# Expert 0's rows gathered from a table in DRAM, and three moves of work around the experts

## The reference

```python
topk_val, topk_idx = jax.lax.top_k(logits, TOPK)
probs = jax.nn.softmax(topk_val, axis=-1)
for kk in range(TOPK):
    idx = topk_idx[:, kk]
    w = probs[:, kk][:, None]
    for e in range(NE):
        mask = idx == e
        eo = _expert(xf, mask, ...)      # LN, 8-head attention, LN, MLP
        out = out + jnp.where(mask[:, None], eo * w, 0.0)
return out.reshape(B, N, E)
```

## Time and profile before

| what | value |
|---|---|
| median of 3 runs | 1327.05 us (1324.7 to 1328.79) |
| the profiled execution's time | 1324.23 us |
| its span | 1322.5 us |
| PE busy | 1046.1 us, 79% of the span |
| DVE busy | 741.1 us, 56% |
| ACT busy | 455.0 us, 34% |
| POOL busy | 322.1 us, 24% |
| granted TensorE clock, mean | 0.897 |

### The profile page before, as it was taken

One profiled execution on the slowest core, in us unless ns is written; L12 is line 12 of the kernel. 1 busy time (PEld: TensorE's weight loads), 2 busy tenths in 40 slices (PEclk: granted clock), 3 DMA queues, 4 the chain that ended last, 5 costly groups with the idle time before them and its releaser, 6 DMA issues.

```text
span 1322.5 us, 19279 instructions
## 1 busy us (share of the span) xinstructions
PE 1046.1 (79%) x5070; PEld 576.6 (44%) x5071; DVE 741.1 (56%) x1573; ACT 455.0 (34%) x843; POOL 322.1 (24%) x298
## 2 busy tenths in 40 slices
PE   1986799998800888778876959979799899989984
PEld 1654467777800333434333424434344344533333
DVE  5395435441461478736784473674856636736854
ACT  1301121221312366225635314434435451235522
POOL 3102324441367144203441020000000124213311
PEclk9987799998555998989897889999999999989998
DMA  5291000000427115121323020000000312120010
GB/s 148 66 285 50 1 2 0 0 0 1 157 60 233 75 48 164 42 78 32 128 85 120 1 63 1 1 0 0 0 0 3 110 48 75 41 70 1 1 31 33
DMA packets 32650, 74.58 MB, mean 56 GB/s; under 512 B 6253, under 2 KB 6551, under 8 KB 32297
## 3 DMA queue, kind: packets, MB, share of 16 engines
q1 hardware_dynamic: 24269, 55.97, 13.6%
q0 software_dynamic: 8000, 15.44, 4.0%
q10 hardware_dynamic: 288, 2.10, 0.4%
HBM read 50.63 MB, written 24.13 MB: 57 GB/s over the span
## 4 chain that ended last, share of the span: by engine, by line
PE 63%; DVE 16%; issue 10%; ACT 5%; POOL 3%; DMA 1%; DVEq 1%; SPq 0%; ACTq 0%; POOLq 0%
PE bank L1334 16%; PE bank L1425 9%; PE bank L1207 8%; PE bank L1246 5%; PE bank L1455 3%; DVE den L2159 3%; PE bank L1510 3%; PE bank L1242 2%; PE bank L1410 2%; PE bank L1389 2%; PE bank L1412 2%; PE bank L1173 2%; POOL lists L658 1%; PE bank L1469 1%; PE bank L1229 1%
## 5 line engine op out<-in xcount | busy, mean ns | idle before, releaser
L1425 PE MATMUL bank<-probs_t,v_head 128*128 128x512 f32 (+1 forms) x288 | 146.9, 593 | 17.0 <-ACT probs_t L991 16.4
L1789 DVE TENSOR_SCALAR oh_src<-iota,edge 125x1250 f16 x178 | 101.2, 568 | 105.4 <-PE bank L1207 100.5
L2072 DVE TENSOR_REDUCE mx<-bank 128x1 f32<-128x512 f32 x144 | 88.2, 656 | 75.7 <-PE bank L1389 74.9
L991 ACT ACTIVATE probs_t<-bank 128x512 f32<-128x512 f32 x144 | 81.6, 574 | 142.3 <-PE bank L1412 130.1
L560 POOL TENSOR_TENSOR w<-w_stage,w 128x1024 f16<-128x1024 f32 x40 | 85.8, 2158 | 145.9 <-ACT w L804 145.8
L1207 PE MATMUL bank<-oh_src,oh_dst 125*125 x534 | 110.8, 357 | 2.8 <-issue 0.4
L1510 PE MATMUL bank<-probs_t,v_head 128*128 128x128 f32 (+2 forms) x192 | 88.8, 549 | 6.9 <-ACT probs_t L1042 5.1
L1334 PE MATMUL bank<-hT,w 128*128 128x256 f16 (+1 forms) x552 | 89.5, 326 | 1.9 <-DVE hT L2005 1.9
L1207 PEld LDWEIGHTS bank<-oh_src,oh_dst 125*125 x534 | 70.2, 142 | 43.5 <-issue 24.2
L1455 PE MATMUL bank<-hT,w 128*128 128x512 f16 x288 | 72.7, 385 | 7.8 <-ACT t L1016 7.8
L1334 PE MATMUL bank<-w,hT 128*128 128x512 f16 x264 | 68.0, 415 | 10.3 <-DVE hT L2005 10.3
(11 more groups left out here) (306 smaller groups left out, 1956.3 us busy)
## 6 DMA issues: line engine op xcount, KB each, us to landing
w_stage<-in_ew_dram SPq DMA_DIRECT2D x40, 512.0 KB, 3.6
lists<-zeros SPq DMA_DIRECT2D x1, 10340.0 KB, 50.2
x_in<-lists SPq DMA_DIRECT2D x20, 517.0 KB, 6.7
x_mem<-lists SPq DMA_DIRECT2D x3, 1024.0 KB, 6.2
x_mem<-lists SPq DMA_DIRECT2D x1, 2560.0 KB, 10.8
out_dram<-x_mem SPq DMA_DIRECT2D x10, 250.0 KB
big<-in_x_dram SPq DMA_DIRECT2D x10, 224.0 KB
x_mem<-in_x_dram SPq DMA_DIRECT2D x1, 2240.0 KB
```

Source lines behind the costliest of these rows:

```text
L991: nc.scalar.activation(probs_t[:, x % NPB, 0:cn], stb[x % 2][:, 0:cn], ACT.Exp).then_inc(s_exp, 1)
L1425: nc.tensor.matmul(pvb[(hd * nq + s) % 2][:, 0:cn], v_head[:, hd, kt, :], probs_t[:, (hd * nx + i) % NPB, 0:cn], start=(k == 0), stop=(k = ...
L1789: nc.vector.tensor_scalar(oh_src[:, bass.ds(slot, 1), i, 0:N].rearrange("p a n -> p (a n)"), iota[:, :], edge[:, 0, i, bass.ds(g, 1)], Non ...
L2072: nc.vector.tensor_reduce(mx[:, hd, t, s:s + 1], sbk[i % 2][:, 0:cn], AX.X, ALU.max).then_inc(s_mx, 1)
```

## The change

1. **A table and a gather for expert 0.** SP writes the first 514 columns of `rows` to a DRAM `table` (10 DMAs of 125 rows, row 0 zero). DVE compares, for each tile, the slot of expert 0 that each row has with the numbers 1 to 1,280 (one-hots `where_a`, `where_b`), PE multiplies them with the rows' numbers `ids` (one column for each 128 slots), and DVE casts the result to `first_rows_i`. POOL gathers four tiles of `x_in` with it. Ahead of that gather go only 2 of the 20 scatters; the other 18 stand in expert 0's arm, ahead of `values_of`. The wait for all of them is on POOL ahead of `second_head(0)`, on DVE at the second pair, on SP ahead of the loads of x1 and of the three last list columns (`s_extra`, awaited by `owners`). `s_routed` is gone.
2. **Marks over 128 partitions.** Ten numbers a partition for each of 16 rows; the write to DRAM has 2,048 runs of 20 bytes.
3. **POOL's and SP's work.** The low halves of expert 0's six first weight pieces are made ahead of `rrstd`, the sixth piece is loaded after x2's sixth tile, most of `total_rows` is cleared early, `bias_rows`, `ones_k` and the rest of `total_rows` after the gathers. SP no longer loads `x_in` for expert 0.
4. **Short arms.** `owners` stands at the third pair (j = 2) in place of the first.
5. **Long arm.** `bias_halves` stands ahead of the maxima; PE spreads the first head's 18 score pieces over value tiles 1 to 9 in place of the last ones (`late`).

```diff
+AHEAD = 4
+SPARE = 2
@@ SP
+            sp.dma_start(table[0:1, :], zeros[0:1, 0:D + 2]).then_inc(s_lists, 16)
...
             for t in range(NT):
                 sp.wait_ge(s_x2, t + 1)
                 sp.dma_start(out_t[:, t, :], x2[:, t, :]).then_inc(s_x2out, 16)
+                if t == NB:
+                    for p in range(WB, QKV_P):
+                        load_piece(0, p)
+            sp.wait_ge(s_rn, 1)
+            sp.wait_ge(s_rr, 2)
+            sp.wait_ge(s_lists, 32)
+            for t in range(NT):
+                sp.wait_ge(s_xf, t + 1)
+                sp.dma_start(table[1 + t * TT:1 + (t + 1) * TT, :], rows[:, t, 0:D + 2]).then_inc(s_lists, 16)
             sp.wait_ge(s_marks, 1)
-            sp.dma_start(marks_dram, marks[:, :, :, :]).then_inc(s_marksout, 16)
-            for p in range(WB, QKV_P):
-                load_piece(0, p)
-            sp.wait_ge(s_x2out, 16 * NT)
+            sp.dma_start(marks_dram.rearrange("e s g (p i) -> p (e s g) i", i=PER),
+                         marks[:, :, :, :, :].rearrange("p e s g i -> p (e s g) i")).then_inc(s_marksout, 16)
             sp.wait_ge(s_marksout, 16)
-            sp.wait_ge(s_scat, 16 * 2 * NT)
-            sp.sem_inc(s_routed, 1)
...
+                sp.wait_ge(s_scat, 16 * 2 * NT)
+                with sp.If(e < 1):
+                    sp.dma_start(x_in[:, :, D + 2:DS],
+                                 lists[0:LIST, D + 2:DS].rearrange("(t p) d -> p t d", p=P)).then_inc(s_extra, 16)
...
-            load_rows(0)
@@ POOL
+            nc.gpsimd.memset(total_rows[:, 2:NTL, :], 0.0).then_inc(s_pch, 1)
...
+            for p in range(QKV_P):
+                low_weights(0, p)
+            pool.wait_ge(s_rmv, 1)
...
-            nc.gpsimd.memset(total_rows[:, :, :], 0.0).then_inc(s_econst, 1)
...
-            for p in range(QKV_P):
-                low_weights(0, p)
-            pool.wait_ge(s_routed, 1)
+            pool.wait_ge(s_lists, 32)
+            scatter(range(SPARE // 2))
+            pool.wait_ge(s_lists, 32 + 16 * NT)
+            pool.wait_ge(s_index, 1)
+            gather(range(AHEAD))
+            nc.gpsimd.memset(total_rows[:, 0:2, :], 0.0).then_inc(s_econst, 1)
...
+                with nc.gpsimd.If(e < 1):
+                    if nt > AHEAD:
+                        pool.wait_ge(s_index, 2)
+                        gather(range(AHEAD, nt))
+                    scatter(range(SPARE // 2, NT))
...
                     values_of(0, 1)
+                    pool.wait_ge(s_scat, 16 * 2 * NT)
                     second_head(0)
@@ PE
+            for i in range(AHEAD):
+                last = tokens_of(i, where_a, i * P, 0)
...
-                    late = max(2, nt // 2)
                     for t in range(1, nt):
                         value(t)
-                        if t >= late:
-                            for i in range((t - late) * nx // (nt - late), (t + 1 - late) * nx // (nt - late)):
-                                scores(0, i)
+                        for i in range((t - 1) * nx // (nt - 1), t * nx // (nt - 1)):
+                            scores(0, i)
@@ DVE
+            one_hots_of(where_a, 0, LW_A)
...
+            dve.wait_ge(s_placed, 1)
+            token_rows(0, AHEAD)
+            one_hots_of(where_b, LW_A, LW_B)
+            one_hots_of(where_a, LW_A + LW_B, LW_B)
...
+                    if j == 1:
+                        dve.wait_ge(s_scat, 16 * 2 * NT)
...
-                    if j == 0:
+                    if j == 2:
                         owners(e, nt)
...
                     split_pair()
+                    bias_halves()
                     for i in range(nx):
                         maximum(0, i)
                     owners(e, nt)
                     second_head_copies()
-                    bias_halves()
+                    dve.wait_ge(s_scat, 16 * 2 * NT)
```

More of the change, by code:

```diff
@@ L58 @@
 UP = 5
+AHEAD = 4
+SPARE = 2
+PER = LW // P
+LW_A = AHEAD * P
+LW_B = (LW - LW_A) // 2
 FAR = -30000.0
@@ L169, in program @@
         lists = dram("lists", (NE * LIST, DS), F32)
+        table = dram("table", (N + 1, D + 2), F32)
         ident = sb("ident", [P, P], F32)
@@ L272, in program @@
         gaps = sb("gaps", [P, 3, NE], F32, route)
-        marks = sb("marks", [NE, 2, 2, LW], F16, route)
+        where_a = sb("where_a", [TT, NT, LW_A], F16, route)
+        where_b = sb("where_b", [TT, NT, LW_B], F16, route)
+        number = sb("number", [TT, LW], F16, route)
+        ids = sb("ids", [TT, NT], F16, route)
+        where = sb("where", [TT, 3, NT], F32, route)
+        first_rows_i = sb("first_rows_i", [P, NTL], I32, route)
         route.close()
@@ L439, in program @@
         s_pref = sem("s_pref")
-        s_tot = sem("s_tot")
+        s_where = sem("s_where")
+        s_placed = sem("s_placed")
+        s_index = sem("s_index")
+        s_extra = sem("s_extra")
+        s_ahead = [sem(f"s_ahead{b}") for b in range(3)]
         s_slots = sem("s_slots")
@@ L1935, in _, with one_hots_of, token_rows @@
             link(nc.vector.tensor_tensor(masked[:, :, :, :], before[:, :, :, :], member[:, :, :, :], ALU.mult))
+            link(nc.vector.tensor_tensor(where[:, 1, :], masked[:, 0, 0, :], masked[:, 1, 0, :], ALU.add))
+            link(nc.vector.tensor_tensor(where[:, 2, :], where[:, 1, :], where[:, 0, :], ALU.add))
+            def one_hots_of(hot, c0, cn):
+                for t in range(NT):
+                    nc.vector.tensor_scalar(hot[:, t, 0:cn], number[:, c0:c0 + cn], where[:, 2, t:t + 1], None,
+                                            ALU.is_equal).then_inc(s_where, 1)
+            def token_rows(i0, i1):
+                nc.vector.tensor_copy(first_rows_i[:, i0:i1], banks[6][:, i0:i1]).then_inc(s_index, 1)
+            one_hots_of(where_a, 0, LW_A)
             for k in range(2):
@@ L1961, in _ @@
+            link(last)
+            link(nc.vector.tensor_tensor(in_grp[:, 1, :, :], in_grp[:, 1, :, :], in_grp[:, 2, :, :], ALU.subtract))
+            both = in_grp[:, 0:2, :, :].rearrange("p g e i -> p e g i")
+            link(nc.vector.tensor_scalar(marks[:, :, 0, :, :], both, BIG, None, ALU.mult))
+            nc.vector.tensor_scalar(marks[:, :, 1, :, :], both, BIG, -BIG, ALU.mult, ALU.add).then_inc(s_marks, 1)
+            dve.wait_ge(s_placed, 2)
+            token_rows(AHEAD, NTL)
             dve.wait_ge(s_arms, 1)
-            dve.wait_ge(s_routed, 1)
```

164 lines of the change are left out of this document (91 added, 73 removed).

## The result

The changed kernel took 1289.41 us (median of 4 runs, 1287.77 to 1292.2), the kernel before 1325.88 beside it: a ratio of 0.9732, interval 0.9713 to 0.9752, 36.5 us faster. Forecast were 1284 with a range of 1272 to 1300. The profiled execution is the slowest of the four (1292.2); its span fell from 1322.5 to 1290.4, by 32.1. I work the terms out on the two traces.

What follows compares the result with a forecast made beforehand. TensorE bounds most of the span, so only its waits pay, the largest 56.5 us. T0 -27.4, slow scatters +2.2, marks 0, owners -4.6, long expert -13.4: -43.2 from 1324.2, 1281.0; with 2.8 for the median 1284, range 1272 to 1300.

Steps and rivals of the forecast that it cites:

- T0: The moment ACT can start on expert 0's gathered rows: from 425.0 to 397.6, 27.4 us earlier (31 to 7).
- owners: Three short experts: moving it off j = 0 removes TensorE's 1.53 wait at the second score row, -4.6 (0 to -4.6).
- the long expert: Spread scores gain 3.4 in the value phase, bias rows first gain 10 in the tail: -13.4, range -8 to -15.
- One sign that I had set for being wrong: Routing chain: the forecast is wrong if the gather starts before 386 or after 396.
- Table: SP's ten writes bind the routing chain, on 5 of 16 DMA engines: landed at 391.3 (387.7 to 407).
- Rival A: The table's rows go slower than x2's writes: 8 us more, 1292, or the whole, 1300; chance 0.2.
- D: The table is not the limit, its writes overlap wider or run faster; scatters bind: -6, 1278; chance 0.06.
- Second head: Expert 0, GpSimd's scatters and copies ready at 435.4 against a need of 436.4; slow scatters +2.2 (0 to 14.5).
- Rival B: GpSimd's scatters are held by VectorE: at half of the 18 about +5, 1289, at all 1296; chance 0.12.
- Marks: Expert 0's marks, behind the table on the engines: ready 406 to 416 against a need of 413.6; 0 (0 to 2.5).
- Rival E: Slower than before: the marks' 20-byte runs are served one after the other, time near 1595; chance 0.03.
- Low weights: GpSimd's six subtractions, 12.5 us, move under VectorE's x2 loop, ending about 1.5 before rrstd is due: 0, up to +3.

Runs made afterwards that it cites:

- t16: The changed kernel with each table write of 125 rows cut in two, of 112 and 13 rows: 1278.57 us, ratio 0.9639.
- hold: The changed kernel with SP holding expert 0's last four weight pieces and marks loads until the four gathers have landed: 1285.27 us, ratio 0.9690.
- t16s0: The changed kernel with table writes cut in 112 and 13 rows and no scatter ahead of the gathers: 1277.98 us, ratio 0.9626.
- owners0: The changed kernel with owners back at the first pair of the short arms: 1293.13 us, ratio 0.9754.
- late: The changed kernel with the long expert's scores put back beside the last value tiles: 1291.85 us, ratio 0.9739.
- ownlate: The changed kernel with the long arm's second-head copies ahead of owners: 1290.20 us, ratio 0.9733.
- best: The changed kernel with the edits of marksfirst and unlocked together: 1272.69 us, ratio 0.9600.
- marksfirst: The kernel t16s0 with, in expert 0, the marks loads ahead of the last four weight pieces: 1277.81 us, ratio 0.9640.
- unlocked: The kernel ownlate with GpSimd's four weight subtractions in the long arm held until owners is done: 1284.44 us, ratio 0.9703.

## Why the prediction was right, and where its sizes were off

The direction, the range and the mechanism held: the routing's chain ended on the table, on a third of the engines, and t16 shows it by removing it. No term gave all that it was put down for, though: T0 20.8 of 27.4, and less behind it, `owners` 1.4 of 4.6, the long expert 10.5 of 13.4. 5.2 us that I had not forecast made up for a part, so that the time is within 5.4 us of the forecast owes something to luck. One sign that I had set for being wrong did appear, by 0.35: the first gather started at 396.35, after 396. Point by point:

- **Table.** Landed at 395.5, forecast 391.3 (upper bound 407). 1.3 of the 4.2 is the later start of the whole stretch. The rate was right (106 to 121 GB/s against 99 to 120); the remaining 3 lie where the engines also had the marks' runs and two scatters (share 0.68 and 0.58 between 385 and 391), for which I had put in 1.5. The 1 us for the first byte in the sum had no row behind it, and no run separates it. Rival A did not happen, nor D: the rate was that of x2's writes. (The range's lower end, 1272, was 2 too low by its own terms: 1278 - 1.6 - 2.2 = 1274.)
- **Gather and T0.** 404.2 in place of 397.6: 4.2 are the table, 1.7 the landing of the second gather, 5.2 and not 3.5 (bound 7.96), and 0.8 that the first gather began that much behind the table's landing and not at it. Then **the step that failed is the one that let ACT start with two tiles and never asked for the other two**: they waited 3.06 more, for the DMA engines that the weights took, which SP issues as soon as the marks are out. hold shows it, worth 3 us by the trace (4 by the medians). By the second head of expert 0 the gain was 15.4 on the trace, 12.0 short of the 27.4 at T0: 6.6 are T0, 3.0 the third and fourth tile, and 2.4 lie in what follows. These 2.4 are as much as the 2.2 that I had put in for slow scatters, but they are something else: the agreement is luck.
- **Second head.** The 2.2 for slow scatters was not needed: 18 went from 403.56 to 430.7, 27.1 against the 26.8 of full pace. Only one took more than 1.3. Rival B did not happen there; the reverse did. VectorE's casts of the normalised tiles, 0.42 in the kernel before, took 0.67 to 0.80 beside the scatters, which with one slow k_both split cost TensorE 0.7. Another 0.9 is the first value product (4.34 in place of 3.46), which had more of its time at the clock's lower level; and 0.9 is a wait for a maximum, behind a split that was slowed by GpSimd's copies, themselves 2.64 late for the scatters' landing (in hold it is gone). Rival B did happen at one place: the first scatter, beside the one-hots, took 3.75, which was hidden under the table.
- **Marks.** No wait in the changed kernel. They landed 12.6 after their issue, longer than the 8.8 that I had as the upper bound of one such transfer; they were issued at 384.3, before the table had landed, and so they were still there within the 392 to 402 forecast. Rival E did not happen. The slack was as small as said: 8 us of earlier T0 brought a wait of 6.36 (t16s0).
- **Low weights.** Nothing, as taken; they ended at 360.1, and `rrstd` was due at 361.9.
- **Owners.** Forecast -4.6, measured 1.4 by owners0's trace (3.4 by the medians, with overlapping intervals): **the term was mis-sized, because a wait on one engine was taken for time of the kernel**. 1.53 was the wait at j = 0 in two experts and 0.55 in the third, so 3.6 at most; the next wait of TensorE grew by 0.9 over the three, and the rest returned in places that I did not follow up.
- **Long expert.** Forecast -13.4 by 3.4 and 10. The stretch fell by 10.5, and with the spread undone (late) it falls by as much. The 3.4 of the value phase were real (4.1 at the last maximum, 3.3 at the copies' end, -22.0 to -25.3) and were given back at the wait for the copies in this trace, where the clock falls behind that wait; where it falls earlier they are kept (3.2). With the bias rows first the products no longer waited (10.27 to 0.33). I had named the copies as what the tail hangs on and had not seen that the spread would make TensorE arrive sooner than they.
- **Not in the forecast.** A gain of 1.5 at the change from expert 0 to 1 and of 3.7 from the long expert's start to its first value tile (VectorE begins 5.12 after its last work there and not 7.05; 4.90 to 5.12 in all changed kernels). SP issues the 2.5 MB load of x1 behind two short ones now, not ahead of them, and the share of the DMA engines at VectorE's start fell from 0.94 (710 to 715) to 0.41 (692 to 697). That this is the cause was only argued; no run separates it.

Terms by the trace: T0 -22.1 against the start of x2, +1.3 that start, +5.4 between T0 and the second head, -2.9 to the start of the long expert, -3.7, -10.5, +0.4 to the end: -32.1. The medians say -36.5; this profile was the slowest execution of its four, 2.8 above their median, and the one before was 1.7 below its own (1325.88 of four executions; the 2.8 in the forecast was of three).

For rival B the Trainium skill, "SBUF — State Buffer", section "🔬 SBUF: two separate sides", says that the port pair which VectorE and GpSimd share is an exclusive lock for a whole instruction. The 2.1 to 2.4 of ownlate's copies beside subtractions of 2.1, and 0.48 without them, agree. For descriptors it came out as the forecast had read the rule, a train of one-hots that holds GpSimd off to its end, in all but one of the thirteen traces with one-hots: the first scatter or gather, issued into the train, ended only behind its last operation (0.36 behind in ten, 0.13 in best, 1.16 in marksfirst), though each operation takes but 0.24. In t16s0 it got through in 1.29 with 2.4 us of the train still to come; why there is not settled. My reading of the rows before, slowing and no full stop, was too mild.

## What to carry to other kernels

Count the DMA engines of a transfer before its bytes: a busy share of 0.33 over a long stretch was a third of the engines at their limit, and cutting 125 rows in 112 and 13 was worth 11 us here. When a transfer is put on the path, ask of everything behind it (all tiles, not the first two) and of what else goes out in the same microseconds. A wait of one engine is worth its length only if no other resource stands as close behind; two edits that shorten the same stretch are to be undone one at a time before both are credited, and the granted clock of the two traces is to be compared first: here it moved the same stretch by 3 us with no edit in it.

## What the runs showed of the hardware that was not expected

- 2,048 DMA runs of 20 bytes (40 KB) landed 12.6 to 13.6 us after their issue where the table and two scatters were still on the engines (the changed kernel, hold), and 5.7 after it in t16s0, issued behind table and gathers. Beside them and the first scatters a gather of 128 rows took 9.3 us from its issue in t16 (5.2 in the changed kernel), with the engines at 0.94 and 79 GB/s; most of that busy time belongs to the gathers' and scatters' own packets. Why they were so slow is not settled.
- VectorE's small operations beside a GpSimd subtraction of 2.1 us took 2.0 to 2.4, 0.17 to 0.49 alone, one for each subtraction.
- A scatter or gather that GpSimd issues beside a train of VectorE operations of 0.24 each ended behind the train in twelve of thirteen traces (3.6 to 3.95 us in place of 1.0 to 1.3). VectorE's casts beside a row of scatters went from 0.42 to 0.80.
- TensorE's granted clock fell to about 0.55 over 5 us (its lower level, 1.2 GHz, for most of them) once behind short idle stretches in the long expert, at one of two places 10 us apart from trace to trace, the same long arm in hold and in the changed kernel included. Behind the wait for the copies it cost about 3 us more than ahead of it (112.6 against 109.4). With quick copies it cost 2.7 even early (best 108.7, against unlocked's 106.1, where it did not happen).
